# A two-layer kernel: key and query projections of both heads at once, from the fifth pair on as three products of high and low parts, with some steps of the routed and state-space stages moved

## The reference

```python
# layer 0, attention: 16 heads of 64
Q = einsum('btd,hkd->bthk', x, W_Q) + b_Q      # K and V the same
scores = einsum('bqhk,bshk->bhqs', Q, K) / sqrt(64)
out = einsum('bqhk,hdk->bqd', softmax(scores) @ V, W_O) + b_O
# layer 0, routed: each token goes to one of 8 experts, 128 -> 512 -> 128, exact gelu, times its gate
# layer 1, state space (256 channels, 16 states):
u  = silu(conv4(x @ fc1.T @ in_proj.T))
dt = softplus(dt_low @ dt_proj.T + dt_b)
h_t = exp(dt_t * A) * h_{t-1} + (dt_t * u_t) * B_t ;  y_t = (h_t * C_t).sum(states)
out = (((y + u * D) * silu(z)) @ out_proj.T) @ fc2.T
# layer 1, dense: 8 experts of 128 -> 256 -> 128, summed, times a gate
```

## Time and profile before

| | us |
|---|---|
| median of 3 runs | 1217.71 |
| range of the runs | 1217.7 to 1219.94 |
| the profiled execution | 1217.61 |
| its span | 1216.3 |
| PE busy (7541 instructions) | 1128.7 |
| DVE busy (1248) | 832.1 |
| POOL busy (410) | 781.9 |
| ACT busy (805) | 583.4 |

### The profile page before, as it was taken

One profiled execution on the slowest core, in us unless ns is written; L12 is line 12 of the kernel. 1 busy time (PEld: TensorE's weight loads), 2 busy tenths in 40 slices (PEclk: granted clock), 3 DMA queues, 4 the chain that ended last, 5 costly groups with the idle time before them and its releaser, 6 DMA issues.

```text
span 1216.3 us, 19302 instructions
## 1 busy us (share of the span) xinstructions
PE 1128.7 (93%) x7541; PEld 660.3 (54%) x7541; DVE 832.1 (68%) x1248; ACT 583.4 (48%) x805; POOL 781.9 (64%) x410
## 2 busy tenths in 40 slices
PE   5899999999999999999999999968788988779998
PEld 2455555555555555555655556956434434335786
DVE  5565567566566566556575556535889889998887
ACT  3434444443443444443434444537864576443654
POOL 4577778677777777767579882272586678883100
PEclk9899999999999999999999999989898989999999
DMA  6000000000000000000000115364463344440000
GB/s 195 2 1 1 1 1 1 2 1 1 2 2 1 2 1 1 2 2 1 1 2 14 51 48 195 100 199 187 157 216 132 118 136 138 147 147 18 9 9 18
DMA packets 38058, 68.83 MB, mean 57 GB/s; under 512 B 5936, under 2 KB 24112, under 8 KB 37968
## 3 DMA queue, kind: packets, MB, share of 16 engines
q1 hardware_dynamic: 32624, 47.75, 12.3%
q0 software_dynamic: 5344, 19.86, 4.7%
HBM read 61.30 MB, written 6.16 MB: 55 GB/s over the span
## 4 chain that ended last, share of the span: by engine, by line
PE 77%; DVE 8%; issue 6%; POOL 6%; ACT 3%; DMA 1%; POOLq 0%; SPq 0%; DVEq 0%; ACTq 0%
PE psum L564 19%; PE psum L533 16%; PE psum L550 6%; PE psum L580 5%; PE psum L537 5%; POOL hc L1937 4%; PE psum L642 3%; PE psum L926 3%; PE psum L845 3%; PE psum L909 3%; PE psum L595 2%; PE psum L615 2%; DVE psum L1632 2%; PE psum L708 2%; DVE hs L1639 2%
## 5 line engine op out<-in xcount | busy, mean ns | idle before, releaser
L1830 POOL TENSOR_TENSOR psums<-psums,prob 128x1024 f32<-128x1024 f32 x180 | 426.6, 2370 | 104.2 <-ACT prob L998 82.7
L1347 DVE TENSOR_REDUCE mx<-psum 128x2 f32<-128x1024 f32 x256 | 302.0, 1220 | 211.2 <-PE psum L550 211.2
L998 ACT ACTIVATE prob<-psum 128x1024 f32<-128x1024 f32 x256 | 243.1, 1025 | 218.2 <-PE psum L537 218.2
L564 PE MATMUL psum<-prob,V 128*64 128x512 f32 x1024 | 258.4, 604 | 0.0
L1937 POOL TENSOR_TENSOR hc<-hs,cc 128x1024 f32<-128x1024 f32 x64 | 151.3, 2364 | 73.9 <-DVE hs L1639 72.7
L1639 DVE TENSOR_TENSOR_SCAN hs<-dA,psum 128x1024 f32<-128x1024 f32 x64 | 146.3, 2287 | 2.7 <-DVE psum L1632 0.7
L845 PE MATMUL psum<-hc,ident 128*128 128x512 f32 x256 | 126.7, 619 | 3.0 <-POOL hc L1937 2.9
L564 PEld LDWEIGHTS psum<-prob,V 128*64 128x64 f32 x1024 | 62.0, 136 | 98.3 <-issue 92.6
L1830 POOL TENSOR_TENSOR psums<-prob 128x1024 f32<-128x1024 f32 x30 | 71.5, 2382 | 62.9 <-ACT prob L998 62.9
L533 PE MATMUL psum<-q_hi,k_hi 64*128 64x512 f32 x512 | 108.4, 419 | 0.0
L537 PE MATMUL psum<-guard,row_one 64*128 64x512 f32 x512 | 101.7, 393 | 2.2 <-DMA guard<-mrow 2.2
(11 more groups left out here) (255 smaller groups left out, 1702.6 us busy)
## 6 DMA issues: line engine op xcount, KB each, us to landing
cc<-C_rows SPq DMA_DIRECT2D x64, 512.0 KB, 3.7
...
```

The lines of the kernel that those rows point to most:

```text
L564: ins = pe.matmul(A.O[HALF[s], :], A.V[pair % 2][:, j, s * DH:(s + 1) * DH], A.prob[unit(pair, c, j) % NPB][:, s * CH:(s + 1) * CH], start ...
L998: act.activation(A.prob[n % NPB][:, :], slots.bank("score", pair, c, j).rearrange("p s n -> p (s n)"), ACT.Exp, scale=float(DH) ** -0.5).t ...
L1347: dve.tensor_reduce(K.A.mx[:, :, t, c], slots.bank("max", pair, t, c), AXX, ALU.max).then_inc(*slots.inc("max", pair, t, c))
L1830: pool.tensor_tensor(total[:, :], (K.A.prob[(n - 1) % NPB] if j == 1 else total)[:, :], K.A.prob[n % NPB][:, :], ALU.add).then_inc(*K.psum ...
```

## The change

Attention: the weights and the normed inputs of keys and queries get a high part (float32r, a copy by ACT) and a low part (a subtraction by POOL), made once, in pair 0 and the start of pair 1, for the second batch entry in pair 4. `pe_proj` no longer issues one matmul for each head into a column half, but both heads at once on the full array: one float32 matmul for pairs 0 to 3, three one-pass matmuls (high by high, high by low, low by high) from pair 4 on.

```diff
 def pe_proj(K, pe, pair, what, c):
     A, work = K.A, K.work
     b, p = divmod(pair, NPAIR)
-    w, bank = A.wk if what == "k" else A.wq, work.bank("proj", pair, what, c)
+    bank, cs = work.bank("proj", pair, what, c), slice(c * CH, (c + 1) * CH)
     if p == 0 and (what, c) == CHUNKS[0]:
         pe.wait_ge(*work.empty("ln", LN_ATTN + b, NT // 4 - 1))
     if pair == 0 and c == 0:
         pe.wait_ge(*K.ld["w" + what])
+    if pair >= SPLIT_FROM and p == SPLIT_FROM * (1 - b) and (what, c) == CHUNKS[0]:
+        pe.wait_ge(A.w_lo_done, 2)
+        pe.wait_ge(A.xn_lo_done, b + 1)
     if work.free("proj", pair, what, c):
         pe.wait_ge(*work.free("proj", pair, what, c))
-    for s in range(2):
-        ins = pe.matmul(bank[HALF[s], :], w[:, (2 * p + s) * DH:(2 * p + s + 1) * DH], K.xnT[:, b, c * CH:(c + 1) * CH],
-                        start=True, stop=True)
+    if pair < SPLIT_FROM:
+        passes = [(A.raw[what], K.xnT[:, b, :])]
+    else:
+        passes = [(A.w_parts[what][i], A.xn_parts[b][j]) for i, j in HI_LO]
+    for i, (w, xn) in enumerate(passes):
+        ins = pe.matmul(bank, w[:, 2 * p * DH:(2 * p + 2) * DH], xn[:, cs], start=(i == 0), stop=(i == len(passes) - 1))
     ins.then_inc(*work.full.inc("proj", pair, what, c))
...
+def act_weights_high(K, act, what):
+
+    act.wait_ge(*K.ld["w" + what])
+    act.copy(K.A.w_parts[what][0][:, :], K.A.raw[what]).then_inc(K.A.w_hi_done, 1)
+
+
+def act_inputs_high(K, act, b):
+    act.wait_ge(*K.work.empty("ln", LN_ATTN + b, NT // 4 - 1))
+    act.copy(K.A.xn_parts[b][0][:, :], K.xnT[:, b, :]).then_inc(K.A.xn_hi_done, 1)
...
+def pool_weights_low(K, pool, what):
+
+    A = K.A
+    hi, lo = A.w_parts[what]
+    pool.wait_ge(A.w_hi_done, 1 + (what == "q"))
+    pool.tensor_tensor(lo[:, :], A.raw[what], hi[:, :], ALU.subtract).then_inc(A.w_lo_done, 1)
+
+
+def pool_inputs_low(K, pool, b):
+    A = K.A
+    hi, lo = A.xn_parts[b]
+    pool.wait_ge(A.xn_hi_done, b + 1)
+    pool.tensor_tensor(lo[:, :], K.xnT[:, b, :], hi[:, :], ALU.subtract).then_inc(A.xn_lo_done, 1)
```

```diff
+RESULTS_AT = {3: (2 * NSLOT - 4, 2 * NSLOT - 3), 5: (2 * NSLOT - 2, 2 * NSLOT - 1)}
...
-    order += [("fetch", s + 13), ("fetch", s + 14), ("silu", 0, 0), ("silu", 0, 1), ("up", s + 8), ("gelu", s + 8), ("down", s + 7), ("yrow", s + 7)]
-    order += [("xpj", 0), ("xpj_take", 0), ("up", s + 9), ("gelu", s + 9), ("pick",), ("xpj_out", 0), ("dtp", 0, 0), ("up", s + 10), ("gelu", s + 10), ("xdr", 0), ("dtp", 0, 1)]
-    order += [("down", s + 8), ("yrow", s + 8), ("dtp_out", 0, 0), ("dtp_max",), ("softexp", 0, 0), ("down", s + 9), ("yrow", s + 9)]
-    order += [("down", s + 10), ("yrow", s + 10)]
-    return order + [("softlog", 0, 0), ("dtp_out", 0, 1), ("dt", 0, 0), ("du", 0, 0)]
+    order += [("fetch", s + 13), ("fetch", s + 14), ("silu", 0, 0), ("up", s + 8), ("down", s + 7), ("silu", 0, 1), ("up", s + 9), ("yrow", s + 7)]
+    order += [("xpj", 0), ("xpj_take", 0), ("gelu", s + 8), ("gelu", s + 9), ("pick",), ("up", s + 10), ("dtp", 0, 0), ("xpj_out", 0), ("gelu", s + 10)]
+    order += [("xdr", 0), ("dtp_out", 0, 0), ("softexp", 0, 0), ("down", s + 8), ("yrow", s + 8), ("dtp", 0, 1), ("dtp_max",), ("down", s + 9), ("yrow", s + 9)]
+    order += [("down", s + 10), ("yrow", s + 10), ("softlog", 0, 0)]
+    return order
...
-           11: [("wback_out", 0), ("wback_out", 1), ("inp", 0, 3), ("readd", 1)], 12: [("inp_out", 0, 3)],
-           13: [("lnvar", 5), ("lnroot", 5)], 14: [("lnrows", 5)], 15: turned(5), 16: [("fc1", 1), ("fc1_out", 1)],
+           11: [("wback_out", 0), ("wback_out", 1), ("readd", 1)],
+           12: [("inp", 0, 3)], 13: [("inp_out", 0, 3), ("lnvar", 5), ("lnroot", 5)], 14: [("lnrows", 5)], 15: turned(5), 16: [("fc1", 1), ("fc1_out", 1)],
...
-           27: [("dtp", 1, 0), ("dtp_out", 1, 0)], 28: [("softexp", 1, 0)], 29: [("softlog", 1, 0), ("dt", 1, 0)], 30: [("du", 1, 0)], 31: [("inp", 1, 2)], 32: [("inp_out", 1, 2)],
...
+           27: [("dtp", 1, 0), ("dtp_out", 1, 0)], 28: [("softexp", 1, 0)], 29: [("softlog", 1, 0), ("dt", 1, 0), ("du", 1, 0)], 32: [("inp", 1, 2)],
...
+    order = [("after", "inputs"), ("gain0",), ("dt", 0, 0), ("du", 0, 0), ("decay", 0), ("dtp_out", 0, 1)]
...
+    if n == SKIP_AT:
         pe.wait_ge(X.skip_done, KI)
         for c in range(NC):
-            pe.matmul(X.Y[:, c * CH:(c + 1) * CH], X.skip[:, k, :], X.u[b][:, k, c * CH:(c + 1) * CH], start=True, stop=False)
+            pe.matmul(X.Y[:, c * CH:(c + 1) * CH], X.skip[:, k, :], X.u[b][:, k, c * CH:(c + 1) * CH], start=False, stop=False)
     pe.wait_ge(X.product_done, u + 1)
     for c in range(NC):
         ins = pe.matmul(X.Y[:, c * CH:(c + 1) * CH], K.ident[:, :], X.hc[u % 3][:, c * CH:(c + 1) * CH],
-                        start=False, stop=(n == NS - 1))
+                        start=(n == 0), stop=(n == NS - 1))
...
-    ins.then_inc(*own.inc())
-    dve.wait_ge(*own.now())
-    dve.tensor_scalar(K.std[:, :], K.mv[:, :, 1], LN_EPS, None, ALU.add).then_inc(K.ln_var, 1)
...
+def dve_gain0(K, dve):
+
     X = K.X
-    if (b, k) != (0, 0):
-        return
-    dve.wait_ge(X.dt_done, 1)
-    dve.tensor_tensor(X.du[b][:, k, :], X.dt[b][:, k, :], X.u[b][:, k, :], ALU.mult).then_inc(X.du_done, 1)
+    dve.wait_ge(X.B_done, 1)
+    dve.tensor_tensor(X.gain[0], X.gain[0], X.u[0][:, 0, :], ALU.mult).then_inc(*K.dve_own.inc())
+    dve.wait_ge(*K.dve_own.now())
```

More of the change, by code:

```diff
@@ L65 @@
 FFN_BANKS = (2, 3, 4, 5)
+HIDDEN = [n % 4 if n >= NSLOT + 5 else 2 + n % 2 for n in range(2 * NSLOT)]
+RESULTS_AT = {3: (2 * NSLOT - 4, 2 * NSLOT - 3), 5: (2 * NSLOT - 2, 2 * NSLOT - 1)}
+SPLIT_FROM = 4
+SKIP_AT = 11
 class Signal:
@@ L322, in recurrence_order @@
     for i in range(0, len(splits), 2):
-        one[46 + i // 2 - i // 20] = one.get(46 + i // 2 - i // 20, []) + splits[i:i + 2]
-    order = [("after", "inputs")]
+        one[47 + i // 2 - i // 20] = one.get(47 + i // 2 - i // 20, []) + splits[i:i + 2]
+    order = [("after", "inputs"), ("gain0",), ("dt", 0, 0), ("du", 0, 0), ("decay", 0), ("dtp_out", 0, 1)]
     for u in range(RECS + 1):
@@ L1056, in act_gelu @@
     R = K.R
-    rows, h = R.wts[BUFFER[n]], R.hT[n % 2]
+    rows, h = R.wts[BUFFER[n]], R.hT[HIDDEN[n]]
     act.wait_ge(*K.work.full.at("up", n))
     act.wait_ge(R.ld_wts[BUFFER[n]], 16 * (USE[n] + 1))
-    if n >= 2:
-        act.wait_ge(*K.work.full.at("down", n - 2))
+    users = [i for i in range(n) if HIDDEN[i] == HIDDEN[n]]
+    if users:
+        act.wait_ge(*K.work.full.at("down", users[-1]))
     for m in range(M0):
@@ L1194, in act_unit @@
     if u == 0:
-        act_decay(K, act, 0)
         act_decay(K, act, 1)
@@ L1629, in dve_unit @@
     dve.wait_ge(X.B_done, u + 1)
-    if n == 0:
+    if u == 1 or (u and n == 0):
         dve.wait_ge(X.du_done, KI * b + k + 1)
-    dve.tensor_tensor(X.gain[u % 2], X.gain[u % 2], X.du[b][:, k, :], ALU.mult).then_inc(X.gain_done, 1)
+    if u == 0:
+        dve.wait_ge(X.dt_done, 1)
+    dve.tensor_tensor(X.gain[u % 2], X.gain[u % 2], (X.du if u else X.dt)[b][:, k, :], ALU.mult).then_inc(X.gain_done, 1)
     if n == 2 and u > NS:
         dve_output(K, dve, *divmod(u // NS - 1, KI))
+    for slot_n in RESULTS_AT.get(u, ()):
+        dve_yrow(K, dve, slot_n)
     dve.wait_ge(X.gain_done, u + 1)
@@ L1796, in pool_root @@
     pool.wait_ge(K.ln_var, n + 1)
+    pool.tensor_scalar(K.std[:, :], K.mv[:, :, 1], LN_EPS, None, ALU.add).then_inc(*own.inc())
+    pool.wait_ge(*own.now())
     if n not in ACT_ROWS:
```

50 lines of the change are left out of this document (32 added, 18 removed).

## The result

The changed kernel takes 1211.70 us (median of 4 runs, 1209.9 to 1212.04) where the kernel before takes 1218.54 (4 runs, 1217.7 to 1219.94): ratio 0.994, 95% interval 0.9922 to 0.9957. Its profiled execution took 1211.87 with a span of 1210.6, against 1217.61 and 1216.3: 5.7 us less by the spans, where the forecast was 11.1 less. By the medians it is 6.8 less. The time lies inside the range of the forecast, 1196 to 1212, at its upper end, and outside the 1203 to 1209 of the forecast's own case.

A forecast was written before the change was run, and what follows sets the result against it. PE was taken to bound attention, and DVE, with what it waits for, the scan and its head; 1217.61 + 3.2 (attention) - 14.3 (scan and head) = 1206.5, own range 1203 to 1209, stated range 1196 to 1212.

The forecast's parts named there:

- The full form's price: Attention from pair 4: entering and leaving the full-array form costs 0.19, a step takes 1.91 against 1.87, +0.04.
- Rivals A: Attention: the full form costs nothing for one-pass groups, first pass to value product 0.70; 1190 to 1195 in all; chance 0.13.
- C: Attention: the three passes write the same bank and run one after another, 2.40 a step, +25, 1229.6; chance 0.04.
- Attention +3.2: Whole attention stage: +1.9 from pair 4 on and +1.3 in pairs 0 to 3 from the projections' form.
- The splits: ACT's copies and POOL's subtractions in attention fit into free time: cost 0, up to 2.4 without that cover.
- The head, -5.5 to the first scan: State-space head: logarithm 4.2 earlier through the gelus (3.20 and 1.0), dt to first scan 1.3 shorter.
- Fourth and fifth scan: Scan start: a later fourth decay gives back 1.3; moving results ahead of the scan gains 2.95 at the fifth.
- Unit 13: Scan: DVE's wait of 1.42 for a spread behind a projection into z goes, as that moves one unit back; -1.4.
- unit 14: Scan: the epsilon's 1.54 on DVE goes to POOL, -1.4, bounds 0 (another step takes over its wait) and 1.5.
- Unit 18, -1.7: Scan: the skip product moves to the twelfth addition, where PE has no such work beside it; -1.7, bounds 0.9 and 1.9.
- Unit 32: Scan: dt*u on POOL moves ahead of one product of C, shortening DVE's wait of 3.36; -2.35.
- Rival B: Head: the gelu of slot 25 then waits for something else, so the 4.2 go; 1211 to 1214; chance 0.14.

The follow-up runs named there:

- the last four: Later runs: kernel before again, routing totals one phase later, old projections from pair 10 on, old projections with z at unit 31; ratios of the changed three 0.9936, 0.9928, 0.9896.
- the first eight experiments: Eight kernels, each the changed kernel with edits or rerun, run beside the kernel before at 1215.6 to 1220.2; they measured 1205.30 to 1217.86.

## Why the prediction came out as it did

**The full form's price (+0.04 a step): right.** 0.88 to 0.90 and 1.01 in every pair, and 0.65 to 0.71 more a pair in float32. Rivals A (0.70) and C (1.2) are refuted by the rows.

**Attention +3.2: wrong, +6.2 in the trace.** The sum of steps was too high, not too low: the prediction named pairs that get shorter as a sign that it is wrong, and pairs 4 to 11 got shorter, by 0.24 together, though each step had its price. In the trace without a fall in pair 12 and without the late start (two hidden buffers), attention ends 0.2 later than with the old projections (756.73 and 756.50): +0.5 at the first column sums, +0.3 in the next pair, and 0.0 to -0.1 in each pair from then on, because a value product elsewhere lost 0.1 twice a pair. It goes with the projection's form in its own phase, as the kernel with old projections from pair 10 on shows; by what mechanism isn't settled, the trace shows no wait for another engine there, before or after. What the prediction left out was the clock. It took attention as one stretch at full clock, and the trace of before has it so from 48 us on (the time up to 17.3 and 6.8 us from 41.2 are slow there too). The fall at the narrow matmuls of pair 12, 3.2 us, came in eight of nine traces with full-form projections and in none of five with the old ones; neither early nor late pairs alone, nor the splits, nor the totals' place is needed for it, and it was missing once. That it goes with this change is what the traces show; by what, is open. The moment at which pair 12 begins divides the traces just as well: 600.3 or later in all those with a fall, 599.7 or earlier in five of the six without one, 600.6 in the sixth. So the form of the projections and a later pair 12 can't be told apart here. A wait there, or the same kernel with its start shifted, wasn't tried.

**The splits cost nothing: right.** Pairs 4 to 11 are not longer, and the kernel without them had no earlier pair.

**The head, -5.5 to the first scan: right in its steps (-4.7 for the gelus, -1.3 for dt to scan), short by 1.9 ahead of them.** The stretch from the last column sums to `xpj` is 1.3 to 2.7 longer than before in all nine traces of changed kernels that ran before the last four. Timeline of PE there, first of the kernel before, then of the changed one:

```profile
817.40 0.66 PE L515 MATMUL psum<-ident,xrows 128*128 128x128 f32 x4 [3.34 <-DVE xrows L1319]
818.78 1.06 PE L719 MATMUL psum<-kq_wts,slot_rows_h 128*128 128x128 f32 x8
821.44 1.05 PE L708 MATMUL psum<-slotT,kq_wts 128*128 128x128 f32 x8
```

```profile
824.02 0.66 PE L525 MATMUL psum<-ident,xrows 128*128 128x128 f32 x4 [3.95 <-DVE xrows L1345]
825.75 1.91 PE L735 MATMUL psum<-kq_wts,slot_rows_h 128*128 128x128 f32 x8
829.52 1.05 PE L724 MATMUL psum<-slotT,kq_wts 128*128 128x128 f32 x8
```

It divides into three parts. From the last column sums to the turn of the normed rows (first row) it takes 61.35 for 60.92; with the epsilon on DVE 60.84. From there to the next `up` (third row) 5.50 for 4.04: the granted clock is at its lower level from 824.7 to 828.1, where the trace of before has 1.00, and eight matmuls of `down` take 1.91 for 1.06. From that `up` to `xpj` 14.95 in both. So of the 1.9, 0.4 is a later turn and 1.5 the clock. The second part is 4.9 to 6.4 in all nine traces, each with such a fall. PE's idle time ahead of it, 3.95 for 3.34, isn't what decides it: in the kernel with the old form in pairs 0 to 3 it was 2.61, and the clock fell too. The earlier trace rows gave the gelu's 3.2 and 1.0; that the buffers brought 2.1 and the order 2.6 is a division that the prediction had otherwise, with a sum of 4.2 for 4.7.

**Fourth and fifth scan: right.** +1.24 for 1.3, 15.98 behind the first for 16.1. Of the results 0.6 stayed visible at unit 5, and unit 6 gave 0.4 back, together 0.2 for 0.1.

**Unit 13 right, unit 14 wrong, unit 12 missed.** Unit 12 gave 1.4 for which the forecast had no term: its spread stood behind eight matmuls of the taps (L761), which in the trace of before ran at the lower clock (901.3 to 904.7; 1.58 us, and the spread 1.20) and after take 1.12 and 0.71 and come 0.6 earlier behind the scan of unit 11. At unit 14, where it counted -1.4 with a bound of 0, the time is +0.4: DVE came 2.95 us earlier to the moments (units 12 and 13), POOL did not (its sum of gathered rows ends 11.4 behind the scan of unit 11 in both traces), and that sum became the wait. The whole, -2.5 for -2.8, came out near by luck. That the epsilon's 1.54 comes back wherever POOL's product runs over it agrees with both traces of the kernel before; what failed is the step from there to -1.4, that no other wait takes its place.

**Unit 18, -1.7: mis-sized, -2.4** with the units behind it. **Unit 32 right**, -2.2. **Unit 34 missed, +1.6**: the move of slot (1, 2) was counted as free. It put a projection ahead of a spread just where the clock falls, and the two together cost what neither does alone.

**The sum.** From `xpj` on -13.8, forecast -14.3; ahead of it +8.1, forecast +3.2. The term that was mis-sized is attention's, +3.2 with +6.2 measured, and in it the assumption of an unchanged clock, 2.2 at the start and 3.2 in pair 12; the same assumption costs 1.5 of the 1.9 ahead of `xpj`. Beside it the profiled execution of before was taken as its median; the 13 and 7 runs of the kernel before beside the first eight experiments have medians of 1219.66 and 1219.91, 2 above it. Rival B had a time close to the result, but its mechanism didn't occur: the gelu's gain went through. The range reaches up to 1212 only for half of B, so that it holds 1211.70 is luck too.
